# A Perceiver block on one core: rstd ahead of the residual additions, w1 in two loads, reordered stage ends

## The reference

```python
x = x + xattn(layernorm(x), ctx, ctx, mask, W_Q, W_K, W_V, W_O)    # 512 context rows per batch, masked
x = x + attn(layernorm(x), Wq, bq, Wk, bk, Wv, bv, Wo, bo)         # within the 64 tokens of a batch
x = x + ffn(layernorm(x), W1, b1, W2, b2)
# attn: scores = Q K^T / sqrt(32); keep the 64 largest per row (there are 64 keys: all); softmax; V; Wo
# ffn:  Wq1 = ternary(W1); Wq2 = ternary(W2); relu(x Wq1^T + b1) Wq2^T + b2   (512 -> 2048 -> 512)
# ternary(W) = clip(round(W / (mean|W| + 1e-5)), -1, 1)
```

## Time and profile before

| | |
|---|---|
| Median of 3 executions | 1710.17 us (1710.16 to 1712.34) |
| Profiled execution | 1712.46 us, its span 1710.6 us |
| Mean granted TensorE clock | 0.974 |

### The profile page before, as it was taken

The page is one execution under the profiler, slowest core; times in us unless marked ns, Lnnn a source line. Parts: engine busy times, 40 slices in busy tenths (PEclk is TensorE's granted clock), DMA queues, the critical chain, the costliest instruction groups (busy, mean ns, idle before and its releaser), DMA issues.

```text
span 1710.6 us, 37206 instructions
## 1 busy us (share of the span) xinstructions
PE 1595.5 (93%) x15244; PEld 1326.3 (78%) x15244; DVE 1144.0 (67%) x1542; ACT 621.5 (36%) x1607; POOL 219.5 (13%) x300
## 2 busy tenths in 40 slices
PE   5899999999999999788889989889799999999999
PEld 4678888888888888667778868778578888888887
DVE  3677777777777778856677677677785456545633
ACT  2655555555555555454222222222212222222221
POOL 1001111000000001310100100100132022202200
PEclk9999999999999999889989999989899999999999
DMA  6144444444444445553233233232521112112110
GB/s 223 38 112 117 119 111 117 121 118 124 113 110 110 110 111 173 185 187 80 66 86 82 76 92 80 74 90 73 139 62 57 57 36 75 49 39 59 38 37 25
DMA packets 138736, 161.39 MB, mean 94 GB/s; under 512 B 13984, under 2 KB 104224, under 8 KB 137376
## 3 DMA queue, kind: packets, MB, share of 16 engines
q1 hardware_dynamic: 138512, 156.11, 33.0%
q10 hardware_dynamic: 144, 4.19, 0.6%
HBM read 67.97 MB, written 25.17 MB: 54 GB/s over the span
## 4 chain that ended last, share of the span: by engine, by line
PE 66%; DVE 15%; DMA 7%; issue 4%; SPq 4%; POOL 2%; ACT 2%; DVEq 0%; POOLq 0%; ACTq 0%
PE project L351 32%; PE project L1387 14%; PE scores L1858 3%; PE scores L1856 3%; PE project L1858 3%; PE project L1856 3%; PE scores L810 3%; SPq L564 2%; DMA x<-self_residual 2%; DVE row_sum L540 2%; PE attended_t L829 2%; DVE self_probs L545 2%; DVE self_probs_blocks L556 1%; DMA cross_probs_t<-cross_scores_probs 1%; DVE self_blocks_t L431 1%
## 5 line engine op out<-in xcount | busy, mean ns | idle before, releaser
L1387 PE MATMUL project<-ff_xt,w_ternary 128*128 128x512 f32 x1024 | 254.7, 391 | 7.7 <-DVE ff_xt L1380 7.7
L1387 PEld LDWEIGHTS project<-ff_xt,w_ternary 128*128 128x128 f32 x1024 | 193.2, 189 | 48.5 <-DVE ff_xt L1380 8.2
L1397 ACT ACTIVATE hidden<-project,b_sb 128x512 f32<-128x512 f32 x128 | 88.2, 689 | 344.1 <-PE project L1387 344.1
L994 ACT ACTIVATE cross_scores_probs<-cross_scores_probs,exp_bias,logit_scale 128x128 f32<-128x128 f32 x256 | 123.0, 482 | 139.1 <-DVE exp_bias L1128 139.1
L351 PE MATMUL project<-self_xt_hi,self_w_hi 128*128 128x256 f32 x512 | 149.9, 293 | 2.8 <-DVE self_w_lo L411 2.4
L351 PE MATMUL project<-self_xt_lo,self_w_hi 128*128 128x256 f32 x512 | 146.3, 286 | 0.0
L351 PE MATMUL project<-self_xt_hi,self_w_lo 128*128 128x256 f32 x512 | 146.1, 285 | 0.0
L994 ACT ACTIVATE cross_probs<-cross_scores,exp_bias,logit_scale 128x128 f32<-128x128 f32 x256 | 122.8, 483 | 4.6 <-DVE exp_bias L1128 4.6
L351 PE MATMUL project<-ctx_hi,cross_w_hi 128*128 128x512 f32 x256 | 105.6, 413 | 15.3 <-DVE ctx_lo L1153 15.3
L351 PE MATMUL project<-cross_w_hi,ctx_hi 128*128 128x512 f32 x256 | 105.5, 412 | 0.0
L351 PEld LDWEIGHTS project<-self_xt_hi,self_w_hi 128*128 128x128 f32 x512 | 99.6, 195 | 6.4 <-issue 3.8
(11 more groups left out here) (173 smaller groups left out, 3931.2 us busy)
## 6 DMA issues: line engine op xcount, KB each, us to landing
ctx_raw<-in_ctx SPq DMA_DIRECT2D x64, 256.0 KB, 3.9
cross_probs_t<-cross_scores_probs SPq DMA_DIRECT2D x128, 128.0 KB, 2.6
cross_probs_t<-cross_scores SPq DMA_DIRECT2D x128, 128.0 KB, 2.7
self_probs_t<-self_probs_blocks SPq DMA_DIRECT2D x128, 128.0 KB, 2.7
cross_xt_raw<-in_x_t SPq DMA_DIRECT2D x64, 128.0 KB, 2.5
cross_x<-in_x SPq DMA_DIRECT2D x32, 256.0 KB, 3.1
x<-cross_x SPq DMA_DIRECT2D x32, 256.0 KB, 2.8
self_x<-x SPq DMA_DIRECT2D x32, 256.0 KB, 2.8
```

The lines of the kernel that those rows point to most:

```text
L994: last = nc.scalar.activation(c_p[buf][:, cols], c_s[buf][:, cols], ACT.Exp, bias=exp_bias[:, buf, g:g + 1], scale=logit_scale[:, parity(u ...
L1387: last = nc.tensor.matmul(PJ[m % 2][:], w1_q[:, c, cols], x_t[parity(v)][:, c].rearrange("p n a r -> p (n a r)"), start=(c == 0 and x_t is ...
L1397: nc.scalar.activation(h_raw[:, m % 2, :], PJ[m % 2][:], ACT.Relu, bias=b1_sb[:, m:m + 1]).then_inc(h_relu, 1)
```

## The change

Four things change. GpSimd's step in the self loop calls `rstd_of` for unit u + 2 ahead of `self_residuals(u + 1)`. The load of w1 is issued in two parts, the first 14 of its 16 row chunks (3.67 MB) behind ScalarE's `self_qk_out(u, "K0")` of the last cross step, the last 2 (0.5 MB) where the whole load stood. In the last cross step VectorE's `a_lo(u, 0)` goes ahead of `divide(u, 2)`. At the end of the self stage VectorE does the division and the blocks of half 1 and a_lo(u, 0) ahead of the first feed-forward statistics, transposes both halves of the first feed-forward unit in the last step but one (the second into `sx[:, 0]`, which is free once the additions of unit 14 are done) and does `a_lo(u, 1)` before the values; in the last step both `ff_x_lo` stand ahead of the division of half 0, and ScalarE's second `ff_x_hi` ahead of the exponentials; SyncE issues both gathers of the feed-forward layer norm in the last step but one. `f_ln_in` becomes two semaphores.

```diff
@@ -329,7 +329,7 @@
         fx_in = sems("fx_in")
         f_stats, f_agg, f_eps, f_rstd, f_xn, f_res = (
             sem("f_stats"), sem("f_agg"), sem("f_eps"), sem("f_rstd"), sem("f_xn"), sem("f_res"))
-        f_ln_t_done, f_ln_in = sem("f_ln_t_done"), sem("f_ln_in")
+        f_ln_t_done, f_ln_in = sem("f_ln_t_done"), sems("f_ln_in")
         fxt_hi_ready, fxt_lo_ready = sem("fxt_hi_ready"), sem("fxt_lo_ready")
         h_full, h_relu, h_hi_ready, h_lo_ready = (
             sem("h_full"), sem("h_relu"), sem("h_hi_ready"), sem("h_lo_ready"))
@@ -612,6 +612,7 @@
 
 
         CROSS_FILLER, PE_FILLER = 0, 0
+        W1_EARLY = 14
 
         class Cross:
             def __init__(self, kt):
@@ -1041,6 +1042,8 @@
                 exponentials(u, 0)
                 self_w_hi(e, 0)
                 self_qk_out(u, "K0")
+                e.dma_start(w_raw[:, 0, 0:W1_EARLY].rearrange("p k n -> p (k n)"),
+                            w1[:, 0:512 * W1_EARLY]).then_inc(fw_in[0], 16)
                 exponentials(u, 1)
                 self_w_hi(e, 2)
                 self_qk_out(u, "Q0")
@@ -1051,7 +1054,8 @@
                 exponentials(u, 3)
 
                 e.wait_ge(C.stored[0], 16 * K.nt * K.units // 2)
-                e.dma_start(w_raw[:, 0].rearrange("p k n -> p (k n)"), w1).then_inc(fw_in[0], 16)
+                e.dma_start(w_raw[:, 0, W1_EARLY:FC].rearrange("p k n -> p (k n)"),
+                            w1[:, 512 * W1_EARLY:]).then_inc(fw_in[0], 16)
                 full(u, "v1", "last")
                 self_x_hi(e, S_SECOND)
                 self_exponentials(e, S_FIRST, 0)
@@ -1231,10 +1235,10 @@
                 self_ln_normalise(e, S_SECOND)
                 self_ln_transpose(e, S_SECOND)
                 maxima(u, 3)
+                if K.nt == 2:
+                    a_lo(u, 0)
                 divide(u, 2)
                 probs_blocks(u, 2)
-                if K.nt == 2:
-                    a_lo(u, 0)
                 self_values_out(u, 0)
                 divide(u, 3)
                 probs_blocks(u, 3)
@@ -1360,19 +1364,27 @@
                                     mean_var[:, t, 0:1], rstd[:, t, :],
                                     ALU.subtract, ALU.mult).then_inc(f_xn, 1)
 
+        def ff_blocks(v, n):
+
+            return sx[:, 0].rearrange("p t d -> p (t d)") if is_unit(v, 0) and n else f_ln_t[:]
+
         def ff_ln_transpose(e, v, n):
             wait(e, f_xn, total(v, FT, 2 * n + 2))
-            wait(e, f_ln_in, total(v, 128, 64 * n))
-            ln_blocks(fxn[n][:], f_ln_t[:]).then_inc(f_ln_t_done, 1)
+            if is_unit(v, 0) and n:
+
+                e.wait_ge(G.res, NT * (S_UNITS - 1))
+            else:
+                wait(e, f_ln_in[1 - n], total(v, 64, 64 * n))
+            ln_blocks(fxn[n][:], ff_blocks(v, n)).then_inc(f_ln_t_done, 1)
 
         def ff_ln_gather(e, v, n):
             wait(e, f_ln_t_done, total(v, 2, n + 1))
-            ln_gather(e, fxn[n][:], f_ln_t, f_ln_in)
+            ln_gather(e, fxn[n][:], ff_blocks(v, n), f_ln_in[n])
 
         fx_chunks = [xn[:].rearrange("p t (a c r) -> p c (t a) r", a=4, r=32) for xn in fxn]
 
         def ff_x_hi(e, v, n):
-            wait(e, f_ln_in, total(v, 128, 64 * n + 64))
+            wait(e, f_ln_in[n], total(v, 64, 64))
             nc.scalar.activation(fxt_hi[parity(v)][:, :, n], fx_chunks[n], ACT.Copy).then_inc(fxt_hi_ready, 1)
 
         def ff_x_lo(e, v, n):
@@ -1426,8 +1438,6 @@
             def step(u, kind):
                 if kind == "full" and not is_unit(u, 0):
                     load_self_x(e, later(u, 2))
-                if kind == "last":
-                    ff_ln_gather(e, F_FIRST, 1)
                 if not is_unit(u, 0):
                     self_probs_gather(e, u, 0)
                     store(later(u, -1), 1, "last_but_one" if kind == "last" else "full")
@@ -1449,7 +1459,8 @@
                         .then_inc(ff_bias_in, 16)
                 self_probs_gather(e, u, 1)
                 if kind == "last_but_one":
-                    ff_ln_gather(e, F_FIRST, 0)
+                    for n in range(2):
+                        ff_ln_gather(e, F_FIRST, n)
                 store(u, 0, kind)
                 if kind == "last":
                     store(u, 1, kind)
@@ -1633,7 +1644,7 @@
                     return
                 w = u.off
                 if first == 0:
-                    e.wait_ge(fw_in[w], 16)
+                    e.wait_ge(fw_in[w], (32, 16)[w])
                 for n in range(first, last):
 
                     wait(e, fw_summed, w * FC + n)
@@ -1642,8 +1653,8 @@
 
             def last_step(u):
                 ff_x_hi(e, F_FIRST, 0)
+                ff_x_hi(e, F_FIRST, 1)
                 self_exponentials(e, u, 1)
-                ff_x_hi(e, F_FIRST, 1)
                 ff_relu(e, F_FIRST, 0)
                 a_hi(u, 0, "last")
                 ff_relu(e, F_FIRST, 1)
@@ -1704,12 +1715,11 @@
 
             def last_step(u):
                 self_maxima(e, u, 1)
-                ff_ln_transpose(e, F_FIRST, 1)
+                ff_x_lo(e, F_FIRST, 0)
+                ff_x_lo(e, F_FIRST, 1)
                 self_divide(e, u, 0)
                 self_probs_blocks(e, u, 0)
-                ff_x_lo(e, F_FIRST, 0)
                 residual(later(u, -1), 1, "last_but_one")
-                ff_x_lo(e, F_FIRST, 1)
                 self_divide(e, u, 1)
                 self_probs_blocks(e, u, 1)
                 a_lo(u, 0)
@@ -1728,20 +1738,21 @@
                 self_probs_blocks(e, u, 0)
                 residual(later(u, -1), 1, "full")
                 self_maxima(e, u, 1)
+                self_divide(e, u, 1)
+                self_probs_blocks(e, u, 1)
+                a_lo(u, 0)
                 ff_ln_statistics(e, F_FIRST)
                 e.wait_ge(f_stats, FT)
                 ff_ln_aggregate(e)
-                self_divide(e, u, 1)
-                self_probs_blocks(e, u, 1)
-                a_lo(u, 0)
                 self_maxima(e, last, 0)
-                for t in range(FT):
-                    ff_ln_normalise(e, F_FIRST, t)
-                ff_ln_transpose(e, F_FIRST, 0)
+                for n in range(2):
+                    for t in range(2 * n, 2 * n + 2):
+                        ff_ln_normalise(e, F_FIRST, t)
+                    ff_ln_transpose(e, F_FIRST, n)
+                a_lo(u, 1)
                 values_out(None, last, 0)
                 residual(u, 0, "last_but_one")
                 values_out(None, last, 1)
-                a_lo(u, 1)
 
             def step(u, kind):
                 v, w = later(u, 1), later(u, 2)
@@ -1794,10 +1805,10 @@
 
         def self_pool(e):
             def step(u, kind):
+                if kind == "full":
+                    rstd_of(e, G.agg, G.eps, G.rstd, later(u, 2), NT, P)
                 if kind != "last":
                     self_residuals(e, later(u, 1))
-                if kind == "full":
-                    rstd_of(e, G.agg, G.eps, G.rstd, later(u, 2), NT, P)
                 if is_unit(u, 0):
                     self_w_lo(e, 3)
                 if kind == "last_but_one":
```

## The result

| | before | changed |
|---|---|---|
| median of 4 executions | 1711.24 us (1710.16 to 1712.34) | 1635.81 us (1632.01 to 1636.81) |
| profiled execution's span | 1710.6 us | 1634.5 us |
| mean granted TensorE clock | 0.974 | 0.988 |

The ratio is 0.9555, with a 95% interval of 0.9537 to 0.9573: 75 us faster. Forecast were 1635.0 us and a range of 1623 to 1658.

What follows compares the result with a forecast made beforehand. The prediction took GpSimd's late rstd, which delays VectorE's normalisation and then TensorE, as setting the self loop's step. Gains of 67.6 - 0.5 + 5.3 + 2.8 = 75.2 us off 1710.2 gave 1635.0 us, range 1623 to 1658.

Steps and rivals of the forecast that it cites:

- part 1: Self loop, 13 steps: rstd ahead of GpSimd's additions shortens each step to 26.99 us, a gain of 67.6 us.
- Slacks: Self loop step: TensorE has 2.7 us in hand at self_at_lo and 0.8 at the gather for O0's last product.
- its extra: Unit 1 of the self loop: 3.5 us beyond a regular step, for weight sum, threshold and ScalarE's magnitudes.
- Rival C: Self loop: rstd is early but something else holds the normalisation; only stage ends gain, 1702 us; chance 0.03.
- A: Self loop: the next wait, gather or additions against normalisation, takes the place; step 28.5 us, total 1655; chance 0.20.
- B: Last cross step: the early w1 part starves its stage's gathers, a loss of 3 us, total 1643; chance 0.10.
- Rival D: Self loop: GpSimd and VectorE hold each other in every step, 16 us slower, total 1726; chance 0.03.
- Cross to self: Last cross step into self stage: w1 in two parts lets TensorE start at 716.2 us, a gain of 5.3 us.
- Unit 0: Self stage's unit 0: unit 1's additions move beside a normalisation, a cost of 0.5 us (0 to 1.1).
- The end of the self stage: Last two self steps: hidden products start 9.4 us earlier, but most holes stay; gain 2.8 us (0 to 5).

Runs made afterwards that it cites:

- e2_all_but_order: The changed kernel with GpSimd's old order restored (additions ahead of rstd): 1704.17 us, ratio 0.9958.
- e6_delay_7us: The changed kernel with fourteen idle GpSimd operations, 7.3 us in all, ahead of rstd in units 2 to 13: 1680.98 us, ratio 0.9821.

## Why the prediction was right

**The loop.** The steps of part 1 are in the rows. The forecast step was 26.99 us; 26.95 and 27.0 were measured, and 353.4 us for the thirteen against 354.4. The method that gave this was to take from the old step only what has a row: the stand of TensorE, and the product time lost to the low clock behind it. Slacks were foreseen as 3.2 us for rstd and under 1 at the gather; 3.1 us of delay cost nothing and 7.3 cost 3.8. Unit 1 took 786.07 - 756.89 = 29.2 us, so its extra is 2.2 and not 3.5, which is the 1 us of difference. Rival C falls, as no normalisation waits for rstd, and so does A, as no step of the loop waits for the gather: the experiment with 7 us of delay shows what A would have looked like. B falls as well: the early part of w1 costs one wait of 2.86 us and the later gather comes sooner. The prediction read the page's slices of the old loop as 7 to 8 tenths, where they are 8 and 9; nothing in the sum goes by them.

**Holds between GpSimd and VectorE.** By the page "SBUF — State Buffer" of the Trainium skill, section "Who interferes with whom", a VectorE instruction with two SBUF inputs and a GpSimd instruction that reads SBUF exclude each other. The prediction said that no row showed it for the division's product. Now two do: 1.69 us at 856.67, beside additions that run from 854.75 to 857.28, and 5.14 us at 741.06. The first is the 0.4 us that the rule gave (0.46), and VectorE's reserve hides it. Rival D, slower by such holds, falls: in most steps one product is held, by 0.2 to 0.7 us, where D needed 5.4 us a step.

**Cross to self** gained 7.2 us for 5.3. The waits came out as forecast (2.86 for 2.4, 3.79 for 3.5), the early part was issued at 685.15 (forecast 684.5), the attend started at 715.80 (716.2). But the last cross step had begun 0.7 us later than before, so counted from its start the attend came 1.1 us earlier than worked out. The forecast had moved GpSimd's additions of unit 1 out of this step, and had priced them in unit 0, but not what their going gives here: the two normalisations that took 2.22 us beside four additions now come behind the two that are left (699.07 to 701.57) and take 0.99.

```profile
702.30 0.99 DVE L468 TENSOR_SCALAR self_x_norm<-self_x,mean_var,rstd 128x512 f32<-128x512 f32 x2
```

With GpSimd's old order, in e2_all_but_order, four additions stand there and the two take 2.24 us. And the clock behind the hole was taken as unchanged: from the attend to the next row_max it is 17.89 us instead of 18.77, 0.9 us less behind a hole of 3.79 instead of 8.75. These two make the difference of 1.9 in this trace. Of the traces with the split it is the shortest: the stretch takes 54.7 to 56.6 us in them and 61.9 to 62.1 in the three without, so the gain is 5.3 to 7.5 us. Without the split the wait is 10.7 us, so it alone is worth the 6 to 7 us that its removal cost.

**Unit 0**: a cost of 0.5 was forecast, a gain of 0.5 came; both are smaller than the scatter of this stretch (22.6 to 24.2 us), so neither is shown. The two normalisations beside the additions took 2.30 us, 1.2 more than alone, as foreseen, and the product's 3.9 us more were not foreseen. Neither shows on the path, for the reason given in the forecast: the gathers behind w2's 4 MB end the unit.

**The end of the self stage** is the step that failed: 2.8 us forecast, 0.4 measured. Up to the last attend it went as worked out, a little late: the first hidden products came 8.7 us earlier against the loop's end (forecast 9.4), the attend of half 0 stood 45.65 us behind the last row_max (45.1), that of half 1 52.53 (51.8). Then the twelve products of O took 4.44 us where those of before took 1245.84 - 1242.97 = 2.87: 1.6 us lost to the clock. The forecast named the hole ahead of the attend and priced only its time. Before, the largest hole lay ahead of the first hidden products, 11.7 us before the last O; in the changed kernel a hole of 5.23 us ends 9.4 us before it. The experiment with the division first takes that hole away and the products are back at 2.86 us. That it is the hole's place and not something else of that order is argued, not shown, and the order alone doesn't fix it: in seven of the nine traces with the changed end the twelve products take 4.43 to 4.46 us, but in two, e2_all_but_order and e6_delay_7us, they take 2.86 behind holes of the same kind (5.29 and 5.23 us; 4.75 and 5.41). There the low clock lies over the products before them instead: from the attend of half 0 the granted clock is 0.50 from 1224.1 to 1228.9 us and from 1201.7 to 1206.9, against 1156.0 to 1159.3 in the changed kernel, and then it stays at 1.00 over the last products. The whole end takes 524.1 and 523.4 us in these two. So the holes cost something in every trace, and which products pay differs between traces for a reason that stays open.

**The sum.** 1635.0 us were forecast and 1635.8 measured. That it is so near is in part luck: against the forecast the loop gained 1.0 us more, the way into the self stage 1.9 more and unit 0 1.0 more, while the end of the stage gained 2.4 less and the first stretch lost 0.7. What carried the forecast is the loop, nine tenths of the gain, and that was right by its mechanism.

## What to carry to other kernels

When one engine has two jobs in a step, put the one whose input comes early and whose result is awaited ahead of the one that waits for a store; the wait of the second then hides itself. To size such an edit, take one step of the old loop and subtract only what has a row: the stand of the bounding engine and the time that its instructions lose behind it; then walk through every other wait and write down how late it may come. When work leaves a place, price what it frees there as well as what it costs where it goes. A hole ahead of TensorE must be priced twice, for its length and for the slower products behind it; here that second price, 1.6 us in seven traces of nine, took most of what a path shortened by 2.0 us had gained.

## What the runs showed of the hardware

A VectorE product of two SBUF operands (1.23 us alone) ended 5.14 us after it started beside a GpSimd subtraction of 4.55 us over 2048 columns that had begun 0.5 us before it, and took 1.69 us beside GpSimd additions; in the kernel before, where that product began first (746.30, the subtraction at 747.12), it kept its 1.23 us; a transpose and a reduction beside the same additions (854.00 and 855.17 us) kept their 1.25 and 1.18 us. An issue on ScalarE's queue left 2.3 us before the copy that stands ahead of it in the program had started (685.15 against 687.46). A wait of 5.99 us for the weights, ahead of a copy in ScalarE's program, became a stand of 4.89 us on TensorE and made the step 7.8 us longer. Where the granted clock was 0.50 behind TensorE's holes, products of 128x512 started every 0.43 us instead of every 0.23 (1166.61 to 1169.16 in the changed kernel, 1160.03 to 1162.52).
